# Experts of 98 tiles spread otherwise over three stages of a graph-network kernel: 43 pairs of tiles beside the gathers, 6 beside the softmax, none beside the combination

## The chip, the cores and the metric

The kernel runs on one core of one Trainium2 chip. The metric is the device time of one execution in microseconds (us); it is the median over several runs. Engines: PE (matrix multiplication), ACT (activation functions), DVE (elementwise vector work and scans), POOL (here mostly the issue of indirect gathers), SP (issue of transfers). Each runs its own instruction stream in order, and streams wait for each other on semaphores.

## The reference

12500 nodes with 256 features. A first layer sums weighted messages over 200000 edges and multiplies by a matrix; then comes a mixture of experts whose gates are made by graph attention over 131072 edges. Cut to what matters here:

```python
h = (x @ W_gat).reshape(M, HEADS, NUM_EXPERTS)          # 4 heads, 4 experts
e = leaky_relu(a_src[src] + a_dst[dst])                  # one per edge and head
ee = exp(e - segment_max(e, dst)[dst])
alpha = ee / segment_sum(ee, dst)[dst]
scores = layernorm(segment_sum(h[src] * alpha, dst) + b_gat).mean(heads)
w = softmax(top_k(scores, 2))
for ei in range(4):
    hh = gelu(x @ W1[ei] + b1[ei])                       # 256 -> 512
    out += g[ei] * (hh @ W2[ei] + b2[ei])                # 512 -> 256
```

All four experts are computed for all nodes, and the gates weigh them at the end. So the experts don't depend on the attention: they may run at any time between the first layer and the final combination.

## The kernel before, in words

The nodes lie in 98 tiles of 128 rows, which are worked in 49 pairs. `build` runs stages one after the other, each its own block with a barrier at its end: layer norm and planning; the first layer's weighted sums with the sort of the attention's edges; `attention_terms`; then the three that the change touches.

**The gather stage**, `gather_and_experts` (L1057 to L1381). POOL issues 1024 gathers of the attention's rows (L1144, 16 to a batch) and then 98 scatters (L1165). Beside it PE, ACT and DVE compute the experts of the first `EARLY_PAIRS` = 39 pairs: per pair and expert a first layer (L1236), Gelu on ACT (L1190), a second layer (L1247), the bias added by DVE (L1321), and a store of 256 KB to `y_dram` from ACT's queue (L1196).

**The softmax stage**, `segment_softmax` (L1384 to L1544). DVE works over the edges in their order by scans: maxima (L1492, L1501), differences, then it asks ACT for two exponentials (the semaphore `s_go`; ACT at L1437 and L1438) and goes on with the weighted sums (L1520, L1526, L1541). Twice DVE needs a carry across the 128 partitions, for which it asks PE to turn a small tile (`turn`, L1450 and L1453): once with 4 rows, `turn(0, HEADS)`, once with 20, `turn(1, ROWF)`. Beside it runs a second form of the experts, a lane made by `late_experts` (L879), for the next `SCAN_PAIRS` = 4 pairs. In this lane ACT does what DVE does in the gather stage (the normalisation at L917, the copies out of PSUM at L927 and L944), and the bias is multiplied in by PE (L1001, before the matmuls of L1003; the first layer is L991, its Gelu L936). The places at which ACT and PE serve DVE are fixed in their programs: ACT does pair 0 of the lane, then waits for DVE's request and does the exponentials, then pairs 1 to 3. PE does pair 0 with the first turn in it, pair 1, pair 2 with the second turn in it, pair 3. Within a pair the turn stands behind the first layer of expert 2 and ahead of the second layer of expert 1 (`between` in `tensor_pair`). The lane works ahead on PE: the first layers of the next pair's experts 0 and 1 are computed while ACT ends the pair before.

**The combination**, `combine` (L1547 to L1787). POOL gathers the sums of each node from `state_dram` (L1648, 98 gathers in three parts of 20, 20 and 58 tiles). For each part DVE makes the gates (L1707 to L1760), with three requests to ACT in it: an exponential (L1658), a square root (L1664), an exponential (L1669). Then it combines: for each pair 8 steps on DVE (L1769) over the four experts' results `ys` and the nodes' values `xs`, which SP loads ahead into 10 slots (L1599, L1600) and stores from (L1608). Ten pairs follow the first part, ten the second, 29 the third. Beside it a third lane, `last`, does the experts of the last 6 pairs, with ACT's requests put by hand between its steps (`places`). SP loads nothing before the lane's first two inputs have come (`wait_begun`), and it loads a late pair only when the lane has stored it (`wait_stored`).

On ACT each change between Gelu, exponential and square root shows in the trace as an ACT_TABLE_LOAD.

Of the kernel before, what the change touches and what calls it, by code (L numbers as in the profile page):

```python
# [45 lines left out]
FB = HID // P  # L46
PAIRS = TILES // 2
N2 = 2 * P
EARLY_PAIRS = 39
SCAN_PAIRS = 4  # L50
ROWF = HE + HEADS
STATE = HE + 2 * HEADS
BIG = 1.5e38
# [1003 lines left out]
def gather_and_experts(nc, sem, edge_index, m):  # L1057


    with ExitStack() as ctx:  # L1060
# [117 lines left out]
        def _(act):  # L1178
# [15 lines left out]
            def store(n, e, i):  # L1194
                act.wait_ge(s_yo, n + 1)
                act.dma_start(m.y_dram.rearrange("(t p) e f -> p t e f", p=P)[:, ds(i * 2, 2), e, :], yo[:, e, :, :]  # L1196
                              ).then_inc(s_st[e], 16)

            def pair(i, k, first=False, last=False):
                for e in range(EXPERTS):  # L1200
                    hidden(i * EXPERTS + e, e, first=first and e < 2)
                    if e == 0 and not last:
                        load(i + 2, k)
                    if e >= 1:
                        store(i * EXPERTS + (e - 1), e - 1, i)
                    elif not first:
                        store(i * EXPERTS - 1, EXPERTS - 1, i - 1)
# [3 lines left out]
            pair(0, 0, first=True)  # L1211
            with act.Fori(0, EARLY_PAIRS // 2 - 1) as u:
                for k in range(2):
                    pair(u * 2 + (k + 1), (k + 1) % 2)
            pair(EARLY_PAIRS - 2, 1, last=True)
            pair(EARLY_PAIRS - 1, 0, last=True)
            store(EARLY_PAIRS * EXPERTS - 1, EXPERTS - 1, EARLY_PAIRS - 1)
            for e in range(EXPERTS):
                act.wait_ge(s_st[e], 16 * EARLY_PAIRS)

# [3 lines left out]
        def _(pe):  # L1224
# [26 lines left out]
            def turn(i):  # L1251
                pe.wait_ge(s_yn, i + 1)
                if not isinstance(i, int) or i >= 1:
                    pe.wait_ge(s_yt, i)
                for t in range(2):
                    for h in range(HALVES):
                        q = pe.transpose(psY[:, h, t * P:(t + 1) * P], yn[:, t, h * P:(h + 1) * P], m.ident[:])
                q.then_inc(s_ty, 1)

            def pair(i, k, first=False):  # L1260
                for e in range(EXPERTS):
                    if e == 2 and not (isinstance(i, int) and i == EARLY_PAIRS - 1):
                        turn(i + 1)
# [120 lines left out]
def segment_softmax(nc, sem, m):  # L1384
# [3 lines left out]
    with ExitStack() as ctx:  # L1388
# [17 lines left out]
        psT, psB = psE[:, 0:2 * P], psE[:, 2 * P:3 * P]  # L1406
        lane = late_experts(nc, sem, ctx, m, "scan", EARLY_PAIRS, SCAN_PAIRS)

# [8 lines left out]
        block = ctx.enter_context(nc.Block())  # L1417
# [14 lines left out]

        @block.scalar
        def _(act):
            lane.scalar(act, 0, 1)
            act.wait_ge(s_go, 1)
            act.activation(decay[:], decay[:], ACT.Exp).then_inc(s_a, 1)  # L1437
            act.activation(by_head(states[:, :, HE:ROWF]), e[:], ACT.Exp).then_inc(s_a, 1)  # L1438
            act.wait_ge(s_go, 2)
            act.activation(tail[:, 1, 0:HEADS], tail[:, 1, 0:HEADS], ACT.Exp).then_inc(s_a, 1)  # L1440
            lane.scalar(act, 1, SCAN_PAIRS)
            lane.wait_stored(act, SCAN_PAIRS)

        @block.tensor
        def _(pe):
            def turn(n, w):

                pe.wait_ge(s_ask, 2 * n + 1)
                for k in range(2):
                    t = pe.transpose(psT[0:w, k * P:(k + 1) * P], tail[:, k, 0:w], m.ident[:])  # L1450
                t.then_inc(s_t, 1)
                pe.wait_ge(s_ask, 2 * n + 2)
                pe.transpose(psB[:, 0:w], carried[0:w, 0:P], m.ident[0:w, 0:w]).then_inc(s_t, 1)  # L1453

            lane.tensor_pair(pe, None, True)
            lane.tensor_pair(pe, 0, True, lambda: turn(0, HEADS))
            lane.tensor_pair(pe, 1, True)
            lane.tensor_pair(pe, 2, True, lambda: turn(1, ROWF))
            lane.tensor(pe, 3, SCAN_PAIRS)

        @block.vector
        def _(v):
# [84 lines left out]
def combine(nc, sem, b_gat, gamma, beta, out, m):  # L1547


    with ExitStack() as ctx:  # L1550
# [4 lines left out]
        SLOTS = 10  # L1555
        ROUNDS = PAIRS // SLOTS
        REST = PAIRS - ROUNDS * SLOTS
# [16 lines left out]
        ge = sb("f_ge", [P, T, EXPERTS])  # L1574
        ys = sb("ys", [P, SLOTS, 2, EXPERTS, FEAT])
        xs = sb("xs", [P, SLOTS, 2, FEAT])
        LATE = EARLY_PAIRS + SCAN_PAIRS
        lane = late_experts(nc, sem, ctx, m, "last", LATE, PAIRS - LATE)
        assert LATE >= PAIRS - REST

        s_c, s_clear = sem("f_const"), sem("f_states_cleared")
        s_got = [sem(f"f_gathered{n}") for n in range(PARTS)]
# [8 lines left out]
        block = ctx.enter_context(nc.Block())  # L1591

        @block.sync
        def _(sp):
            for n, a in enumerate((b_gat, gamma, beta)):
                sp.dma_start(vec[:, n, :], a.rearrange("(o c) -> o c", o=1).to_broadcast([P, HE])).then_inc(s_c, 16)

            def load(i, k):
                sp.dma_start(ys[:, k, :, :, :], y_t[:, ds(i * (2 * SLOTS) + 2 * k, 2), :, :]).then_inc(s_in[k], 16)  # L1599
                sp.dma_start(xs[:, k, :, :], x1_t[:, ds(i * (2 * SLOTS) + 2 * k, 2), :]).then_inc(s_in[k], 16)  # L1600

            def store(i, k):
                sp.wait_ge(s_done, i * SLOTS + (k + 1))
                if isinstance(i, int) and i * SLOTS + k == PAIRS - 1:
                    sp.dma_start(out_t[:, T - 2, :], xs[:, k, 0, :]).then_inc(s_out[k], 16)
                    sp.dma_start(out[FULL_TILES * P:NODES, :], xs[0:LAST_ROWS, k, 1, :]).then_inc(s_out[k], 16)
                else:
                    sp.dma_start(out_t[:, ds(i * (2 * SLOTS) + 2 * k, 2), :], xs[:, k, :, :]).then_inc(s_out[k], 16)  # L1608

            def refill(i, k):  # L1610
                sp.wait_ge(s_out[k], i * 16)
                if isinstance(i, int) and i * SLOTS + k >= LATE:
                    lane.wait_stored(sp, i * SLOTS + k - LATE + 1)
                load(i, k)

            def round_(i):

                fixed = isinstance(i, int)
                for k in range(SLOTS):
                    if fixed and i * SLOTS + k >= PAIRS:  # L1620
                        return
                    store(i, k)
                    if k >= 2 and not (fixed and (i + 1) * SLOTS + k - 2 >= PAIRS):
                        refill(i + 1, k - 2)
                    if k < 2 and not (fixed and (i == 0 or (i + 1) * SLOTS + k - 2 >= PAIRS)):
                        refill(i, SLOTS + k - 2)

            lane.wait_begun(sp)
            for k in range(SLOTS):
                if k == SLOTS // 2:  # L1630
                    sp.wait_ge(s_got[0], 16 * PART[1])
                load(0, k)
            round_(0)
            with sp.Fori(1, ROUNDS - 1) as i:
                round_(i)
            round_(ROUNDS - 1)
            round_(ROUNDS)
            for k in range(SLOTS):
                sp.wait_ge(s_out[k], 16 * (ROUNDS + (k < REST) + (k == REST - 1)))
# [12 lines left out]
        @block.scalar  # L1652
        def _(act):
            def weights(n):

                a, b = PART[n], PART[n + 1]
                act.wait_ge(s_go, 3 * n + 1)
                act.activation(w1[:, a:b, :], w1[:, a:b, :], ACT.Exp).then_inc(s_a, 1)  # L1658
                act.activation(w0[:, a:b, :], w0[:, a:b, :], ACT.Exp).then_inc(s_a, 1)

            def deviation(n):
                a, b = PART[n], PART[n + 1]
                act.wait_ge(s_go, 3 * n + 2)
                act.activation(one[:, 1, a:b], one[:, 1, a:b], ACT.Sqrt, bias=m.eps[:, 0:1]).then_inc(s_a, 1)  # L1664

            def gate(n):
                a, b = PART[n], PART[n + 1]
                act.wait_ge(s_go, 3 * n + 3)
                act.activation(ge[:, a:b, :], ge[:, a:b, :], ACT.Exp).then_inc(s_a, 1)  # L1669


            places = [[(0, 1), (0, 2), (0, 3)], [(1, 3), (2, 0), (2, 1)], [(3, 1), (3, 2), (3, 3)]]
            pairs = PAIRS - LATE
            between = [{} for _ in range(pairs)]
            for n in range(PARTS):
                for f, (u, place) in zip((weights, deviation, gate), places[n]):
                    between[u][place] = lambda f=f, n=n: f(n)
            lane.scalar_pair(act, None, True)
            for u in range(pairs):
                lane.scalar_pair(act, u, u < pairs - 1, between[u])  # L1680
            lane.wait_stored(act, pairs)

        @block.tensor
        def _(pe):
            lane.tensor(pe, 0, PAIRS - LATE)

        @block.vector
        def _(v):
# [122 lines left out]
```

## Time and profile before

| what | us |
|---|---|
| median of 3 runs (4309.44 to 4312.2) | 4310.04 |
| profiled execution, its own time | 4316.67 |
| its span, first to last instruction | 4315.1 |
| PE busy in the span | 3097.8 (72%) |
| POOL busy | 2801.6 (65%) |
| DVE busy | 1853.2 (43%) |
| ACT busy | 711.1 (16%) |

All times in rows are microseconds from the start of the span of one profiled execution, unless marked ns. In a line of the timeline stand: start, duration, engine, line of the kernel, operation, what it writes and reads, the number of instructions merged into it, and in brackets how long the engine had been idle and what ended that. In the view of stretches each engine has its busy time and, in brackets, its instructions, in the order PE, PE's weight loads, DVE, ACT, POOL; then come the granted clock of PE as a share of full speed, the share of DMA and its GB/s. Durations of matmuls overlap where several are merged. A row with DMA_INDIRECT on POOL is the issue of a gather, not its transfer.

### The profile page before, as it was taken

To read this page: it belongs to the slowest core of one execution; us is meant where nothing else is said; L and a number is where in the kernel's file an instruction comes from. 1 tells how busy PE (TensorE), PEld (TensorE's weight loads), DVE (VectorE), ACT (ScalarE), POOL (GpSimd) and SP (SyncE) were. 2 spreads that over 40 slices of the span, in tenths; PEclk is the share of its full clock that TensorE was granted. 3 is DMA by queue.
4 is the path that set the end of the run, shared out by engine and by line. 5 is a ranking of instruction groups with operands and counts; after the bars stand their busy time and mean duration, and the time that the engine had idled before them with its cause. 6 is when DMAs were issued, how large, how long until landed. Compare 5 with 4: busy or idle time off the path is not lost. (4 is left out here: it accounts for less than half of the span.)

```text
span 4315.1 us, 59490 instructions
## 1 busy us (share of the span) xinstructions
PE 3097.8 (72%) x13541; PEld 2436.0 (56%) x13542; DVE 1853.2 (43%) x4572; ACT 711.1 (16%) x1985; POOL 2801.6 (65%) x2958
## 2 busy tenths in 40 slices
PE   1356666677787887889979999999999400166846
PEld 0234444455555665666658888888888300144634
DVE  5233344534545456433333444444431000188648
ACT  4000000000111111122222222222222000031412
POOL 0677777777777777777747777777777777500860
PEclk6677778877878888998979999999999755588978
DMA  7533333333333433444422222222222110003749
GB/s 245 160 101 101 104 104 107 109 109 111 111 112 114 117 116 115 120 120 124 125 89 61 60 61 63 61 61 63 58 63 61 37 17 10 28 22 137 284 164 348
DMA packets 298222, 449.93 MB, mean 104 GB/s; under 512 B 61256, under 2 KB 232339, under 8 KB 297491
## 3 DMA queue, kind: packets, MB, share of 16 engines
q0 software_dynamic: 114144, 216.61, 19.2%
q1 hardware_dynamic: 83238, 137.78, 8.8%
q10 hardware_dynamic: 100749, 94.40, 6.7%
q8 instruction: 48, 0.79, 0.1%
q14 instruction: 43, 0.35, 0.0%
HBM read 330.48 MB, written 105.96 MB: 101 GB/s over the span
## 5 line engine op out<-in xcount | busy, mean ns | idle before, releaser
L519 POOL DMA_INDIRECT rows<-feats,idx x1564 | 1506.7, 963 | 546.6 <-issue 508.5
L665 PE MATMUL node_sums<-rows,hot 128*128 x3904 | 1122.3, 446 | 480.0 <-SPq L502 458.3
L665 PEld LDWEIGHTS node_sums<-rows,hot 128*128 128x128 f32 x3904 | 832.6, 221 | 728.5 <-issue 592.2
L1144 POOL DMA_INDIRECT got<-row_dram,d_idx x1024 | 994.4, 971 | 356.7 <-issue 306.1
L709 DVE TENSOR_SCALAR hot<-iota,rel,ew_t 128x128 f32<-128x128 f32 x1952 | 556.0, 362 | 64.7 <-DVE rel L705 1.9
L705 DVE TENSOR_SCALAR rel<-dst_t,step_base 128x4 f32 x488 | 123.6, 253 | 1061.3 <-PE node_sums L665 1005.9
L1236 PE MATMUL d_hidden<-d_yt,w 128*128 128x256 f32 x2496 | 569.0, 381 | 0.8 <-DVE d_yt L1336 0.8
L1247 PE MATMUL d_expert<-w,hid 128*128 128x256 f32 x2496 | 564.0, 379 | 0.0
L1247 PEld LDWEIGHTS d_expert<-w,hid 128*128 128x128 f32 x2496 | 474.2, 190 | 64.5
L1236 PEld LDWEIGHTS d_hidden<-d_yt,w 128*128 128x128 f32 x2496 | 470.5, 191 | 62.7 <-DVE d_yt L1336 1.2
L1321 DVE TENSOR_TENSOR yo<-d_expert,b2r 128x512 f32<-128x512 f32 x156 | 107.9, 692 | 708.5 <-PE d_expert L1247 708.5
L1190 ACT ACTIVATE hid<-d_hidden,b1c 128x256 f32<-128x256 f32 x624 | 261.9, 470 | 886.4 <-PE d_hidden L1236 882.0
L573 ACT COPY sums<-node_sums 128x256 f32<-128x256 f32 x98 | 36.5, 373 | 1770.6 <-PE sums_turned L657 1770.6
L980 PE MATMUL scan_ps_y_turned<-ident,scan_y 128*128 128x128 f32 x16 | 2.9, 313 | 371.4 <-ACT scan_y L917 371.4
L980 PEld LDWEIGHTS scan_ps_y_turned<-ident,scan_y 128*128 128x128 f32 x16 | 2.2, 160 | 372.1 <-ACT scan_y L917 371.8
L1648 POOL DMA_INDIRECT ns<-state_dram,last_pos x98 | 156.2, 1593 | 30.4 <-issue 29.6
L1311 DVE TENSOR_TENSOR hot_lo<-iota_b,lo 128x512 bf16<-128x512 bf16 x256 | 159.4, 693 | 0.0
L1769 DVE SCALAR_TENSOR_TENSOR xs<-ys,sc,xs 128x256 f32<-128x256 f32 x392 | 156.2, 480 | 5.6 <-DMA xs<-x_dram 5.0
L1481 DVE COPY decay<-adfirst 128x4 f32<-128x4 f32 x1 | 0.2, 166 | 369.0 <-DMA adfirst<-adst_dram,dst_first 369.0
L1644 POOL MEMSET ns<- 128x2352 f32 x1 | 2.1, 2057 | 237.0 <-POOLq L1388 237.0
L1311 DVE TENSOR_TENSOR hot_hi<-iota_b,hi 128x392 bf16<-128x392 bf16 x256 | 124.9, 562 | 0.0
L653 PE MATMUL x_product<-w_t,sums_t 128*128 128x256 f32 x400 | 124.8, 443 | 0.0
(295 smaller groups left out, 2861.4 us busy)
## 6 DMA issues: line engine op xcount, KB each, us to landing
ys<-y_dram SPq DMA_DIRECT2D x49, 1024.0 KB, 9.8
y_dram<-yo ACTq DMA_DIRECT2D x156, 256.0 KB, 2.2
rows<-feats,idx POOLq DMA_INDIRECT x1564
got<-row_dram,d_idx POOLq DMA_INDIRECT x1024
feats<-xout SPq DMA_DIRECT2D x14, 896.0 KB, 4.9
x_dram<-x ACTq DMA_DIRECT2D x98, 128.0 KB
xs<-x_dram SPq DMA_DIRECT2D x49, 256.0 KB, 10.6
x_ring<-in_x ACTq DMA_DIRECT2D x97, 128.0 KB
```

The lines of the kernel that those rows point to most:

```text
L519: pool.indirect_dma_start(rows[:, k, j, :], None, feats, bass.IndirectOffsetOnAxis(ap=idx[:, half, k, j:j + 1], axis=0)).then_inc(s_got[k] ...
L653: t = pe.matmul(psX[:, 0:FEAT], sums_t[:, k * P:(k + 1) * P], w_t[:, k, :], start=False, stop=(k == HALVES - 1))
L665: t = pe.matmul(psA[:, ds(((code >> 1) & 1) * 512, FEAT)], hot[:, r, j, :], rows[:, ds((code >> 2) & (RING - 1), 1), j, :], start=False, s ...
L705: v.tensor_scalar(rel[:, r, :], m.dst_t[:, ds(g * GT, GT)], m.step_base[:, ds(s, 1)], None, ALU.subtract).then_inc(s_rel, 1)
L709: t = v.tensor_scalar(hot[:, r, j, :], m.iota[:], rel[:, r, j:j + 1], m.ew_t[:, ds(g * GT + j, 1)], ALU.is_equal, ALU.mult)
L1144: pool.indirect_dma_start(got[:, k, j, 0:ROWF], None, m.row_dram, bass.IndirectOffsetOnAxis(ap=idx[:, k, j:j + 1], axis=0)).then_inc(s_got ...
L1190: t = act.activation(hid[:, e % 2, 2 * q + f, :], psL[(e % 2) * 2 + q][:, f, :], ACT.Gelu, bias=b1c[:, e, 2 * q + f:2 * q + f + 1])
L1236: t = pe.matmul(psL[(e % 2) * 2 + q][:, f, :], w1[:, h, e, (2 * q + f) * P:(2 * q + f + 1) * P], yt[:, k, h, :], start=(h == 0), stop=(h = ...
L1247: q = pe.matmul(psO[e % 2][:, t, :], hid[:, e % 2, f, t * P:(t + 1) * P], w2[:, f, e, :], start=(f == 0), stop=(f == FB - 1))
L1311: o = v.tensor_tensor(t[:, a:a + STRIP, :], iota_b[:, None, 0:wide].to_broadcast([P, STRIP, wide]), part[:, ds(q * HCOLS + a, STRIP)][:, : ...
L1648: pool.indirect_dma_start(ns[:, t, :], None, m.state_dram, bass.IndirectOffsetOnAxis(ap=m.last_pos[:, t:t + 1], axis=0), bounds_check=GEDG ...
L1769: q = v.scalar_tensor_tensor(xs[:, k, t, :], ys[:, k, t, e, :], sc[:, ds(i * (2 * SLOTS) + (2 * k + t), 1), e], xs[:, k, t, :], ALU.mult, ...
```

## The change

`EARLY_PAIRS` goes from 39 to 43 and `SCAN_PAIRS` to the rest, 6. The lane of the combination is taken out, with SP's two kinds of waits for it, and ACT serves the gates of each part directly. In the softmax stage ACT now does two pairs ahead of the exponentials (`lane.scalar(act, 0, 2)`) and four behind them; PE does pair 0 with the first turn, pairs 1 to 3, pair 4 with the second turn, and pair 5.

```diff
-EARLY_PAIRS = 39
-SCAN_PAIRS = 4
+EARLY_PAIRS = 43
+SCAN_PAIRS = PAIRS - EARLY_PAIRS
...
         @block.scalar
         def _(act):
-            lane.scalar(act, 0, 1)
+            lane.scalar(act, 0, 2)
             act.wait_ge(s_go, 1)
             act.activation(decay[:], decay[:], ACT.Exp).then_inc(s_a, 1)
             act.activation(by_head(states[:, :, HE:ROWF]), e[:], ACT.Exp).then_inc(s_a, 1)
             act.wait_ge(s_go, 2)
             act.activation(tail[:, 1, 0:HEADS], tail[:, 1, 0:HEADS], ACT.Exp).then_inc(s_a, 1)
-            lane.scalar(act, 1, SCAN_PAIRS)
+            lane.scalar(act, 2, SCAN_PAIRS)
             lane.wait_stored(act, SCAN_PAIRS)
...
             lane.tensor_pair(pe, None, True)
             lane.tensor_pair(pe, 0, True, lambda: turn(0, HEADS))
-            lane.tensor_pair(pe, 1, True)
-            lane.tensor_pair(pe, 2, True, lambda: turn(1, ROWF))
-            lane.tensor(pe, 3, SCAN_PAIRS)
+            lane.tensor(pe, 1, 4)
+            lane.tensor_pair(pe, 4, True, lambda: turn(1, ROWF))
+            lane.tensor(pe, 5, SCAN_PAIRS)
...
-        LATE = EARLY_PAIRS + SCAN_PAIRS
-        lane = late_experts(nc, sem, ctx, m, "last", LATE, PAIRS - LATE)
-        assert LATE >= PAIRS - REST
...
                 sp.wait_ge(s_out[k], i * 16)
-                if isinstance(i, int) and i * SLOTS + k >= LATE:
-                    lane.wait_stored(sp, i * SLOTS + k - LATE + 1)
                 load(i, k)
...
-            lane.wait_begun(sp)
             for k in range(SLOTS):
...
-            places = [[(0, 1), (0, 2), (0, 3)], [(1, 3), (2, 0), (2, 1)], [(3, 1), (3, 2), (3, 3)]]
-            pairs = PAIRS - LATE
-            between = [{} for _ in range(pairs)]
             for n in range(PARTS):
-                for f, (u, place) in zip((weights, deviation, gate), places[n]):
-                    between[u][place] = lambda f=f, n=n: f(n)
-            lane.scalar_pair(act, None, True)
-            for u in range(pairs):
-                lane.scalar_pair(act, u, u < pairs - 1, between[u])
-            lane.wait_stored(act, pairs)
-
-        @block.tensor
-        def _(pe):
-            lane.tensor(pe, 0, PAIRS - LATE)
+                weights(n)
+                deviation(n)
+                gate(n)
```

## Rows read from the trace of the kernel before

**Rows 1.** Busy time by stage: stage, its us, busy per engine, granted clock, DMA share.

```profile
2240.00:3389.00 1149.00, 1147.05 (x6177) 1011.46 (x6175) 438.58 (x793) 261.92 (x624) 850.53 (x911) 1.00 0.24 61
3389.00:3741.00 352.00, 0.00 (x0) 0.00 (x0) 0.53 (x1) 0.00 (x0) 257.16 (x299) 0.51 0.08 12
...
3751.00:3989.00 238.00, 149.60 (x598) 111.56 (x598) 208.49 (x146) 58.80 (x97) 1.00 (x1) 0.80 0.21 84
3989.00:4315.00 326.00, 220.50 (x888) 165.50 (x888) 216.12 (x545) 88.85 (x168) 158.21 (x99) 0.83 0.72 263
```

**Rows 2.** The same view: two equal stretches of the gather stage.

```profile
3200.00:3380.00 180.00, 179.03 (x844) 157.42 (x843) 27.49 (x52) 41.98 (x100) 131.53 (x147) 1.00 0.24 60
3400.00:3580.00 180.00, 0.00 (x0) 0.00 (x0) 0.00 (x0) 0.00 (x0) 131.81 (x146) 0.50 0.10 17
```

**Rows 3.** Timeline around the first request to ACT: start, us, engine, line, [idle<-releaser].

```profile
3816.65 0.59 ACT L944 COPY scan_expert_out<-scan_ps_expert 128x512 f32<-128x512 f32 x1 [4.51 <-PE scan_ps_expert L1003]
...
3817.81 1.28 ACT L1437 ACT_TABLE_LOAD   x1 [0.57 <-ACT scan_expert_out L944]
...
3829.94 3.62 ACT L1437 ACTIVATE decay<-decay 128x4096 f32<-128x4096 f32 x1 [10.85 <-DVEq L1512]
...
3843.92 17.22 DVE L1520 TENSOR_TENSOR states<-states 128x16384 f32<-128x16384 f32 x1 [5.91 <-ACT tail L1440]
3843.93 1.28 ACT L936 ACT_TABLE_LOAD   x1
3845.22 3.03 ACT L936 ACTIVATE scan_hidden<-scan_ps_hidden,b1c 128x256 f32<-128x256 f32 x8
...
3847.99 3.57 PE L1003 MATMUL scan_ps_expert<-w,scan_hidden 128*128 128x256 f32 x8
...
3852.11 1.99 PE L1003 MATMUL scan_ps_expert<-w,scan_hidden 128*128 128x256 f32 x8
```

**Rows 4.** Timeline of the rest of the softmax stage.

```profile
3876.78 0.59 ACT L944 COPY scan_expert_out<-scan_ps_expert 128x512 f32<-128x512 f32 x1 [4.51 <-PE scan_ps_expert L1003]
...
3889.02 3.62 PE L991 MATMUL scan_ps_hidden<-scan_y_turned,w 128*128 128x256 f32 x16
...
3915.97 0.60 PE L1450 MATMUL e_turn<-ident,tail 128*20 128x128 f32 x2 [23.33 <-DVEq L1467]
...
3933.69 46.57 DVE L1541 TENSOR_TENSOR_SCAN states<-decay,states 128x256 f32<-128x256 f32 x60
...
3973.20 0.59 ACT L944 COPY scan_expert_out<-scan_ps_expert 128x512 f32<-128x512 f32 x1 [4.51 <-PE scan_ps_expert L1003]
...
3989.43 2.06 POOL L1644 MEMSET ns<- 128x2352 f32 x1 [237.02 <-POOLq L1388]
```

**Rows 5.** Timeline of ACT in the combination: one copy in successive pairs, undisturbed.

```profile
4221.38 0.59 ACT L944 COPY last_expert_out<-last_ps_expert 128x512 f32<-128x512 f32 x1 [3.28 <-PE last_ps_expert L1003]
...
4256.02 0.59 ACT L944 COPY last_expert_out<-last_ps_expert 128x512 f32<-128x512 f32 x1 [4.26 <-PE last_ps_expert L1003]
```

**Rows 6.** Timeline of the combination: the first burst on DVE and the gathers.

```profile
4041.03 31.75 DVE L1769 SCALAR_TENSOR_TENSOR xs<-ys,sc,xs 128x256 f32<-128x256 f32 x80
...
4044.27 29.39 POOL L1648 DMA_INDIRECT ns<-state_dram,last_pos  x1 [0.30 <-issue]
```

**Rows 7.** Timeline of DVE in the combination: gates of the second and third part.

```profile
4077.86 0.27 DVE L1707 TENSOR_TENSOR seg_keep<-ns,has_edges 128x80 f32<-128x80 f32 x1 [5.08 <-DMA ns<-state_dram,last_pos]
...
4179.16 0.40 DVE L1707 TENSOR_TENSOR seg_keep<-ns,has_edges 128x232 f32<-128x232 f32 x1 [51.44 <-DMA ns<-state_dram,last_pos]
...
4211.72 0.40 DVE L1757 TENSOR_TENSOR f_ge<-f_ge,src_sorted 128x232 f32<-128x232 f32 x1 [3.73 <-ACT f_ge L1669]
```

**Rows 8.** DMA of the last 103 us: GB/s in 40 slices; queue, packets, MB.

```profile
GB/s 0 0 288 362 381 339 424 399 401 414 403 400 408 397 411 389 410 414 390 420 401 403 408 403 411 402 402 410 398 415 408 395 417 404 395 417 377 383 158 6
...
q10 hardware_dynamic: 2176, 2.10, 5.8%
```

**Rows 9.** Waits of the same stretch: us in total, times, longest.

```profile
DVE xs L1769 <- DMA xs<-x_dram: 5.0, 7, 1.2
```

## The prediction

> **What bounds the kernel now.** I read the stages first: busy time per engine in the stretches between the barriers [rows 1]. From the gather stage on there are three, and each has its own limit. In the gather stage PE does the experts of 39 pairs in 1149 us (29.5 us a pair) and then does nothing for 352 us, while POOL issues gathers to the end: POOL sets its length. In the softmax stage (238 us) DVE is busy 208 us and everything else much less, so DVE's chain of scans sets it, with whatever DVE has to wait for. In the combination (326 us) no engine is full; there one must look at what DVE waits for, which is the timeline's to tell [rows 6, 7].
>
> The question for each moved pair is therefore not how much work it is, since that is the same everywhere, but which queue it stands in and what waits behind it.
>
> **Gather stage: four more pairs, cost 0.** Four pairs at 29.5 us are 118 us on PE, which is idle for the last 352 us of the stage [rows 1]; ACT and DVE are idle there too. Could they slow POOL? Two stretches of 180 us show 147 POOL instructions with 131.53 us busy beside the experts and 146 with 131.81 us alone [rows 2]. That is no difference, so I take 0 and keep 2 us as the upper end (one instruction in 146, over 118 us, would be under 1 us; I double it for the stores). Below zero nothing is possible: POOL gains nothing from it. The stage would still have over 230 us of idle PE as cover.
>
> **Softmax stage, first part: one pair now stands ahead of the exponentials.** Before, ACT does one pair, then waits for DVE's request. Its last copy of that pair starts at 3816.65, the table load for the exponential at 3817.81, and the exponential itself only at 3829.94, after 10.85 us of waiting for DVE [rows 3]. So ACT was early by 10.85 us. The change puts a second whole pair in between. How long is a pair of this lane? Not 29.5 us, since it also multiplies the bias in on PE; the same copy of two successive pairs, with no request between them, lies 4256.02 - 4221.38 = 34.64 us apart [rows 5]. The copy that ends the second pair thus starts at 3816.65 + 34.64 = 3851.29. From the copy's start to the table load's end are 3817.81 + 1.28 - 3816.65 = 2.44 us [rows 3], so the exponential starts at 3853.7 in place of 3829.94: **23.8 us later**. DVE has nothing to do meanwhile: already before it waited 5.91 us for ACT there [rows 3], and all its later steps of this stage follow from the exponentials. In short: a pair's 34.64 minus ACT's slack of 10.85. The lower bound is 20.7 us, from the nearest shorter row, 31.6 us from the first hidden block to the last copy in the pair after the exponentials (3876.78 - 3845.22, with two blocks already done ahead); the upper is 26, if PE starts the pair slowly (eight matmuls in 3.57 us in place of 1.99 [rows 3], some more of them).
>
> The Trainium skill (page "ScalarE: Activation LUTs", section "What ACT_TABLE_LOAD costs") states about 2.66 us for a switch of table, 1.38 us of it a drain; the rows show 1.28 us and an ACTIVATE 0.01 us behind the load [rows 3], with no drain. By the page the delay would be 25.2 us, by the rows 23.8; the measurement decides.
>
> **Softmax stage, second part: DVE's question to PE comes while PE is busy.** PE turns DVE's tails for it at a fixed place in its program: after the third layer-1 block of a pair. Before, that was the second pair after the exponentials. PE was ready at 3889.02 + 3.62 = 3892.64 and DVE asked at 3915.97, so PE waited 23.33 us for DVE [rows 4]. Now the turn stands in pair 4, the third pair after the exponentials. The pair after the exponentials (pair 2 now) ends with its copy at 3876.78 + 23.8 = 3900.6; pair 3 takes 34.64 more, to 3935.2; from the copy to the end of the third block are 3892.64 - 3876.78 = 15.86 us, so PE reaches the turn at 3951.1. DVE asks at 3915.97 + 23.8 = 3939.8. So DVE now waits **11.3 us** more: PE's 23.3 us of slack minus one pair of 34.64. Together the softmax stage grows by 35.1 us.
>
> Is DVE's chain still what ends the stage? Its last scan ended at 3933.69 + 46.57 = 3980.26, ACT's last copy started at 3973.20 [rows 4]. Behind the turn both programs are as before (the rest of one pair, then the last pair), so both move by 35.1 and keep their distance of 7 us. The combination's first instruction goes from 3989.43 [rows 4] to about 4024.5.
>
> **Combination: six pairs leave, gain 8 us.** This stage looks like the place to win, since 6 pairs of PE work and their transfers go. But its path runs through POOL. DVE's first part of gates waits for 20 gathers; a burst of 80 combining steps follows, 31.75 us; during it one gather on POOL takes 29.39 us, and it ends 0.9 us behind the burst [rows 6]. The second round shows the same pattern, so there are two such stalls. DVE waited 5.08 us for gathers before the second gates, and 51.44 us before the third [rows 7]. A burst that starts earlier stops POOL earlier for as long, so the third gates still start when 98 gathers and two stalls are over: same distance from the stage's start. What the experts delayed in the first two parts is swallowed by these two waits: gain 0.
>
> Two things remain. In the third gates DVE waited 3.73 us for an exponential that stood behind an expert's copy on ACT [rows 7]; about 0.5 us must stay (the 0.40 us exponential and its semaphore), so 3.2 us are won. Then 29 pairs are combined to the end with DMA at some 405 GB/s [rows 8] and DVE waiting 5.0 us for loads, 7 times [rows 9]. The experts' stores there are 2.10 MB [rows 8], 2.10 / 0.405 = 5.2 us of transfer, and no more than DVE's 5.0 us of waits can be won. Sum 3.2 + 5.0 = 8.2; I take 8, with 3 as the lower end (nothing of the waits) and 12 as the upper (the start of the stage gets its loads earlier and something of it lasts).
>
> **The sum.** Gather 0, softmax +23.8 + 11.3, combination -8: **+27.1 us**. The profiled execution took 4316.67 us (span 4315.1, the rest lies around it), so it would be 4343.8; the median of the runs is 6.6 us lower at 4310.04, which makes 4337. A measurement of this kernel can tell about 0.2% (8.6 us) from no change. The ends: softmax 32 to 38 (twice a pair of 33 to 36 us, less the two slacks of 10.85 and 23.33), gather 0 to 2, combination -12 to -3, so 4330 to 4347; the corners will hardly meet, so 4331 to 4344 is the forecast's own range.
>
> **Rivals.**
> (a) *Only the first delay counts.* If PE gets to the turn no later than DVE asks, the 11.3 us go and 23.8 - 8 = 15.8 remain: 4326. For it: this step is a difference of two estimated times. Against: it needs a pair in PE's 23.33 us of slack [rows 4] in place of 34.64.
> (b) *Faster: the stalls of POOL were made by the transfers.* Place: the two gathers of 29 us [rows 6]. If they come from full DMA queues, and lifting the experts' traffic frees them, the third gates start as soon as the second burst is over, 51.44 us earlier [rows 7]: 35.1 - 8 - 51.4 = -24.3, so 4286. It decides from 36 of the 51 us on. Against: the stall ends with the burst, within 1 us, and the loads of the experts' results, which are most of the traffic, stay.
> (c) *No change: DVE's chain has cover in the softmax.* If the requests to ACT and PE were off the path that ends the stage, only -8 would be left: 4302, within 0.2%. Against: before the first exponential ACT waited for DVE, and behind the last one DVE for ACT [rows 3], so the chain passes through both. That the change doesn't do what it says gives the same time: that would be the pair ahead of the exponentials overlapping with DVE's work after all.
> (d) *PE at its lower clock.* After a pause the eight matmuls of L1003 took 3.57 us, later 1.99 [rows 3]. The granted clock over the softmax stage is 0.80 [rows 1], between the levels 1.2 and 2.4 GHz. If pair 1 and pair 3 run half at the lower level, each gains 34.64 x 0.8 / 2 = 14 us; both are on the path: 4365. Against: PE idles less than before, not more.
>
> **How the numbers follow.** Forecast 0.75; (a) 0.12, (b) 0.04, (c) 0.04, (d) 0.05. The range takes in the forecast's and (a)'s times, 4325 to 4345, and leaves out (b), (c), (d) and the forecast's far corners. Slower: forecast, (a), (d) = 0.92; same: (c) 0.04; faster: (b) 0.04.
>
> **What would show it.** In the profile of the changed kernel: the exponential of the softmax stage with no wait of ACT for DVE before it, 24 us later relative to the stage's start; DVE waiting some 11 us for PE at the second turn, where PE waited before; some 273 us for the stage in place of 238; in the combination two stalls of about 29 us on POOL as before and the third gates 190 us from its first instruction; no wait for loads in the last pairs. POOL's rate beside the experts unchanged, and PE busy until about 3507 us. The prediction is wrong if the stalls shrink, if the turn finds PE waiting, or if the gathers' stage grows.

## The result and the profile after

The changed kernel took 4342.05 us (median of 4, 4339.08 to 4344.24) against 4311.02 us (4309.44 to 4312.2; four runs, one more than the prediction had): a ratio of 1.0072, 95% interval 1.0054 to 1.0089. So it is slower by 31 us, with 23 to 38 us inside the interval. The forecast was 4337, range 4325 to 4345. The profiled execution took 4339.08 us.

First the stages. Stretches between the barriers of the changed kernel, with the columns of [rows 1]:

```profile
2240.00:3389.00 1149.00, 1148.03 (x6191) 1013.12 (x6190) 438.06 (x792) 263.06 (x628) 850.61 (x911) 1.00 0.27 61
3389.00:3500.00 111.00, 108.53 (x509) 95.22 (x507) 15.49 (x26) 25.14 (x60) 80.99 (x92) 1.00 0.27 61
3500.00:3741.00 241.00, 0.00 (x0) 0.00 (x0) 0.00 (x0) 0.00 (x0) 173.45 (x206) 0.51 0.07 8
3748.00:4020.00 272.00, 215.68 (x894) 162.79 (x894) 208.50 (x146) 80.73 (x144) 0.99 (x1) 0.89 0.22 83
4020.00:4337.00 317.00, 0.00 (x0) 0.00 (x0) 215.48 (x545) 12.42 (x19) 157.21 (x99) 0.50 0.67 246
```

PE now works on in the gather stage to about 3500 us and is idle for the last 241 us; before, it was idle for 352 [rows 1]. POOL's busy time in that stage is within 3 us of what it was (1105 us, before 1108). The softmax stage got longer, the combination shorter, and PE is not used in it at all.

The lengths of the stages come from the first instruction of each: POOL's L1126 at 2228.69 us (before 2232.25), the gather L1430 at 3748.00 (before 3751.41), and POOL's clearing of `ns` (L1638 now) at 4020.68.

| stage | before | after | forecast of the difference | measured |
|---|---|---|---|---|
| ahead of the gather stage | 2232.3 | 2228.7 | 0 | -3.6 |
| gather | 1519.2 | 1519.3 | 0 | +0.1 |
| softmax | 238.0 | 272.7 | +35.1 | +34.7 |
| combination, to the span's end | 325.7 | 316.4 | -8 | -9.3 |

The timeline of the softmax stage, the places that answer to [rows 3]:

```profile
3847.82 0.58 ACT L944 COPY scan_expert_out<-scan_ps_expert 128x512 f32<-128x512 f32 x1 [4.44 <-PE scan_ps_expert L1003]
...
3849.10 1.28 ACT L1437 ACT_TABLE_LOAD   x1 [0.70 <-ACT scan_expert_out L944]
3850.40 3.62 ACT L1437 ACTIVATE decay<-decay 128x4096 f32<-128x4096 f32 x1
...
3854.05 4.42 DVE L1515 TENSOR_TENSOR decay<-decay,seg_keep 128x4096 f32<-128x4096 f32 x1 [27.54 <-ACT decay L1437]
```

The exponential (L1437) follows its table load at once: no wait for DVE, where ACT had waited 10.85 us. DVE waits for it, 27.54 us before L1515 (before, 3.74). Measured from the stage's start the exponential comes at 3850.40 - 3748.00 = 102.4 us, before at 3829.94 - 3751.41 = 78.5: 23.9 us later (forecast 23.8).

And the second turn, on DVE, beside [rows 4]:

```profile
3935.80 0.23 DVE L1532 TENSOR_SCALAR cin<-tail,whole 128x4 f32<-128x4 f32 x1
...
3947.91 0.41 DVE L1469 COPY tail_t<-e_turn 20x256 f32<-20x256 f32 x1 [11.60 <-PE e_turn L1450]
...
3964.94 46.57 DVE L1541 TENSOR_TENSOR_SCAN states<-decay,states 128x256 f32<-128x256 f32 x60
```

DVE waits 11.60 us for PE's turned tile; the first turn of the same kernel, for which nobody is late, costs DVE 0.74. So 10.9 us are new (forecast 11.3).

The combination, beside [rows 7]:

```profile
4108.56 0.24 DVE L1691 TENSOR_TENSOR seg_keep<-ns,has_edges 128x80 f32<-128x80 f32 x1 [7.97 <-DMA ns<-state_dram,last_pos]
...
4209.42 0.40 DVE L1691 TENSOR_TENSOR seg_keep<-ns,has_edges 128x232 f32<-128x232 f32 x1 [51.46 <-DMA ns<-state_dram,last_pos]
...
4238.77 0.40 DVE L1741 TENSOR_TENSOR f_ge<-f_ge,src_sorted 128x232 f32<-128x232 f32 x1 [0.52 <-ACT f_ge L1663]
```

From the stage's start the third gates begin at 4209.42 - 4020.68 = 188.7 us (before 189.7), and DVE's wait ahead of them is 51.46 us as before. The wait for the last exponential (L1741) is down from 3.73 to 0.52 us. POOL is still stopped twice:

```profile
4072.47 28.98 POOL L1642 DMA_INDIRECT ns<-state_dram,last_pos  x1 [0.30 <-issue]
...
4129.84 28.99 POOL L1642 DMA_INDIRECT ns<-state_dram,last_pos  x1 [0.30 <-issue]
```

### The profile page after: what moved, and what is told of

Same layout as the page of the kernel before. It is cut to its first block and busy times, and to the rows that moved or that the text cites. A ratio compares the mean times of both kernels' runs of the same rounds, so it can differ in the third digit from the quotient of the medians.

```text
span 4337.1 us, 59587 instructions
## 1 busy us (share of the span) xinstructions
PE 3038.5 (70%) x13477; PEld 2407.6 (56%) x13478; DVE 1868.4 (43%) x4600; ACT 682.3 (16%) x1947; POOL 2798.8 (65%) x2958
## 5 line engine op out<-in xcount | busy, mean ns | idle before, releaser
L1236 PE MATMUL d_hidden<-d_yt,w 128*128 128x256 f32 x2752 | 626.8, 381 | 0.8 <-DVE d_yt L1336 0.8
L1247 PE MATMUL d_expert<-w,hid 128*128 128x256 f32 x2752 | 621.9, 379 | 0.0
L1247 PEld LDWEIGHTS d_expert<-w,hid 128*128 128x128 f32 x2752 | 522.9, 190 | 71.1
L1236 PEld LDWEIGHTS d_hidden<-d_yt,w 128*128 128x128 f32 x2752 | 518.8, 191 | 69.1 <-DVE d_yt L1336 1.2
L1321 DVE TENSOR_TENSOR yo<-d_expert,b2r 128x512 f32<-128x512 f32 x172 | 119.0, 692 | 804.9 <-PE d_expert L1247 804.9
L1190 ACT ACTIVATE hid<-d_hidden,b1c 128x256 f32<-128x256 f32 x688 | 288.2, 470 | 972.4 <-PE d_hidden L1236 972.4
L1638 POOL MEMSET ns<- 128x2352 f32 x1 | 2.1, 2058 | 271.7 <-POOLq L1388 271.7
L1165 POOL DMA_INDIRECT adst_first<-sdat,sidx x98 | 96.3, 982 | 38.2 <-issue 26.9
```

Source lines behind the costliest of these rows:

```text
L1190: t = act.activation(hid[:, e % 2, 2 * q + f, :], psL[(e % 2) * 2 + q][:, f, :], ACT.Gelu, bias=b1c[:, e, 2 * q + f:2 * q + f + 1])
L1236: t = pe.matmul(psL[(e % 2) * 2 + q][:, f, :], w1[:, h, e, (2 * q + f) * P:(2 * q + f + 1) * P], yt[:, k, h, :], start=(h == 0), stop=(h = ...
L1247: q = pe.matmul(psO[e % 2][:, t, :], hid[:, e % 2, f, t * P:(t + 1) * P], w2[:, f, e, :], start=(f == 0), stop=(f == FB - 1))
```

## The experiments

Twelve runs, each beside the kernel before on the same chip. They fell on four chips, and on two of these the kernel before takes about 5800 us and not 4310, with the same program. Ratios of runs on different kinds of chip must not be mixed; so each experiment names the time of the kernel before. Where a delay of some 10 or 20 us is asked for, the ratio alone says little, since its interval on the slower chips is some 17 to 22 us wide; the length of the stage in the trace carries the reading.

**One delay at a time.** The first run takes from the change only ACT's second pair ahead of the exponentials, with 39, 4 and 6 pairs as before:

```diff
-            lane.scalar(act, 0, 1)
+            lane.scalar(act, 0, 2)
...
-            lane.scalar(act, 1, SCAN_PAIRS)
+            lane.scalar(act, 2, SCAN_PAIRS)
```

> The kernel before, with one thing of the change alone: ACT does two pairs of the softmax lane ahead of the exponentials, two behind them. Theory (a pair's 34.6 us less ACT's slack of 10.9, and PE's turn still waits for DVE): +23.8 us, so a ratio of 1.0055, the combination unchanged. Rival (the exponentials are covered by other work of DVE): no difference, 1.000.

Measured: ratio 1.0052 (1.0034 to 1.0071), before 5810 us; by the medians 27.7 us. POOL's wait through the softmax stage in the trace of this run, and ACT's rows in it:

```profile
L1644 POOL MEMSET ns<- 128x2352 f32 x1 | 2.1, 2059 | 263.4 <-POOLq L1388 263.4
```

```profile
5311.58 1.28 ACT L1437 ACT_TABLE_LOAD   x1 [0.70 <-ACT scan_expert_out L944]
5312.87 3.62 ACT L1437 ACTIVATE decay<-decay 128x4096 f32<-128x4096 f32 x1
```

POOL has nothing to do between its first instruction of the softmax stage and the combination, so its idle time, 263.4 us, is the stage's length. In the order of before it is 237.2 us on this chip (the trace of 45/4/0 below) and 237.02 in [rows 4]: +26.2 us. The rival (exponentials covered) is out.

The second run moves only PE's second turn by one pair:

```diff
-            lane.tensor_pair(pe, 1, True)
-            lane.tensor_pair(pe, 2, True, lambda: turn(1, ROWF))
-            lane.tensor(pe, 3, SCAN_PAIRS)
+            lane.tensor(pe, 1, 3)
+            lane.tensor_pair(pe, 3, False, lambda: turn(1, ROWF))
```

> The kernel before, with the other thing alone: PE's second turn stands in the last of the four pairs, one pair later. Theory (34.6 us of a pair less PE's slack of 23.3): DVE waits 11.3 us for the turn, +11.3 us, ratio 1.0026. Rival (only the first delay counts): 1.000. Second rival (two delays overlap in the changed kernel and each alone is larger): over +15.

Measured: ratio 1.0026 (1.0011 to 1.0041), before 5810 us; by the medians 11.1 us. POOL's wait through the stage, and ACT's exponential:

```profile
L1643 POOL MEMSET ns<- 128x2352 f32 x1 | 2.1, 2057 | 250.0 <-POOLq L1388 250.0
```

```profile
5254.52 3.62 ACT L1437 ACTIVATE decay<-decay 128x4096 f32<-128x4096 f32 x1 [8.47 <-DVEq L1511]
```

+12.8 us, with the exponentials where they were (78.6 us from the stage's start, before 78.5). Rival (a), that only the first delay counts, is out.

Why 26.2 and not 23.8 in the first run? ACT's slack is not a constant of the kernel. With the lane's order of before it was 10.85 us in [rows 3], 8.47 here, and 8.20, 10.92 and 7.87 in the three traces of 45/4/0 below (here the last two of them):

```profile
5445.45 3.62 ACT L1437 ACTIVATE decay<-decay 128x4096 f32<-128x4096 f32 x1 [10.92 <-DVEq L1512]
...
3831.53 3.62 ACT L1437 ACTIVATE decay<-decay 128x4096 f32<-128x4096 f32 x1 [7.87 <-DVEq L1512]
```

The second pair keeps its length (5310.30 - 5275.66 = 34.64 in the first run), but the last copy of the lane's first pair comes 65.2 to 69.0 us after the stage's start: 65.2 in [rows 3] and in the changed kernel, 67.8 in the first run. These 2.5 us more are what the first run lost beyond the forecast. It doesn't go with the kind of chip: the slack of 7.87 was seen where the kernel before takes 4316 us, that of 10.92 where it takes 5802. Why the first pair ends earlier or later was not tried. The changed kernel and its variants with the same softmax stage show both delays together: in six traces the exponentials come 23.9 to 27.7 us later, and DVE waits 10.8 to 11.1 us more at the second turn. On this chip the changed kernel lost 272.6 - 237.2 = 35.4 us (trace below), less than 26.2 + 12.8, with a first pair that ended after 65.8 us; both delays are on the path.

**The combination's part alone.** 45 pairs beside the gathers, the softmax stage as before with 4, none beside the combination:

```diff
-EARLY_PAIRS = 43
+EARLY_PAIRS = 45
...
-            lane.scalar(act, 0, 2)
+            lane.scalar(act, 0, 1)
...
-            lane.tensor(pe, 1, 4)
-            lane.tensor_pair(pe, 4, True, lambda: turn(1, ROWF))
-            lane.tensor(pe, 5, SCAN_PAIRS)
+            lane.tensor_pair(pe, 1, True)
+            lane.tensor_pair(pe, 2, True, lambda: turn(1, ROWF))
+            lane.tensor(pe, 3, SCAN_PAIRS)
```

(against the changed kernel). It ran three times, and the changed kernel twice more. First, on the chip of the two runs above:

> The combination's part of the change alone: 45 pairs beside the gathers, the softmax stage word for word as before with 4 pairs, none beside the combination. Theory (softmax cost is all of the loss, combination gains 8 to 9, two more pairs beside the gathers cost nothing): -9 us, ratio 0.998. Rival (stores and loads of 45 pairs slow the gathers): 0 or slower, with a longer gather stage.

> The changed kernel unaltered, beside the three others. The three changed stages of the two traces differ by 25.4 us in sum, the medians by 31. Theory (chance between executions, outside these stages): ratio 1.006 to 1.007, that is +25 to +29. Rival (a cost outside the changed stages): 1.0072 again, and the sum of x1, x2 and x3 (+26) falls short of it by 5 us.

Measured, before 5810 us: 45/4/0 at 1.0218 (1.0197 to 1.024), the changed kernel at 1.0177 (1.0158 to 1.0196). Both expectations missed by far: by the medians 45/4/0 is 118 us slower where 9 us faster was expected, and nothing in the trace of before let one expect it. What the changed kernel's run was to tell, whether a cost lies outside the changed stages, it could not tell here. The trace of the changed kernel on this chip, stretches of its gather stage (from 2655 to 5307 us):

```profile
3000.00:3500.00 500.00, 99.45 (x191) 48.61 (x191) 12.77 (x23) 8.38 (x20) 343.45 (x380) 0.50 0.12 19
3500.00:4000.00 500.00, 97.81 (x188) 47.24 (x188) 14.08 (x26) 8.38 (x20) 340.68 (x378) 0.50 0.12 19
...
4300.00:4700.00 400.00, 400.00 (x2231) 353.40 (x2230) 170.59 (x311) 90.47 (x216) 0.00 (x0) 1.00 0.13 44
```

For 500 us at a time PE executes some 190 matmuls, then, without any change in its program, 2231 in 400 us. The timeline where the one turns into the other:

```profile
4086.57 0.94 POOL L1144 DMA_INDIRECT got<-row_dram,d_idx  x1 [0.30 <-issue]
4087.20 0.59 PE L1247 MATMUL d_expert<-w,hid 128*128 128x256 f32 x1 [2.21 <-issue]
4087.81 0.95 POOL L1144 DMA_INDIRECT got<-row_dram,d_idx  x1 [0.30 <-issue]
...
4090.00 0.59 PE L1247 MATMUL d_expert<-w,hid 128*128 128x256 f32 x1 [2.21 <-issue]
...
4092.80 0.59 PE L1247 MATMUL d_expert<-w,hid 128*128 128x256 f32 x1 [2.21 <-issue]
...
4094.91 4.42 PE L1247 MATMUL d_expert<-w,hid 128*128 128x256 f32 x10 [1.52 <-issue]
```

Each single matmul of 0.6 us stands behind 2.2 us of idle time that nothing in the profile explains ("issue"), until some 7 us after POOL has begun the last of its 1024 gathers (4087.81); from 4094.91 on there are ten in 4.4 us. The granted clock, 0.50 in the slow stretch, doesn't make the gaps: the matmul itself takes only 0.6 us of each 2.8. POOL's own gathers still follow one another every 1.25 us. The same holds for the combination, where the lane stood beside gathers: from L1644 (5472.4 us) to the span's end (5845.1) the first run, with the lane, takes 372.7 us, 45/4/0 without it 5925.9 - 5597.8 = 328.1. So on this chip the engines beside POOL hardly advance while it issues gathers, the 43 pairs are done mostly behind the gathers, and PE ends the stage at 5307 us, with POOL idle before it (875 us ahead of its scatters, which need DVE's plan, and 213.8 ahead of L1430). There every pair moved into this stage costs its full time. The stages of the traces: gather 2546.1 us with 39 pairs (first run), 2662.6 with 43, 2707.8 with 45. That is 29 us a pair for the first four and 27 for all six; the second run, with the same 39 pairs as the first, shows 2535.5, so such a figure is good to 2 or 3 us. For 45/4/0 the stages add up: 162 us more in the gather stage and 45 less in the combination than the first run, 117 against the 118 of the medians over before.

Then both again on another chip, and all 49 pairs beside the gathers:

> 45 pairs beside the gathers, 4 beside the softmax in the order of before, none beside the combination, once more: on the chip of the first four runs the kernel before itself took 5810 us, and PE came to the end of the gather stage long after POOL. Theory: where POOL sets the gather stage (the kernel before near 4310 us), the gather stage keeps its 1519 us, the softmax stage its 238, the combination loses 9: -9 us, ratio 0.998. Where PE sets it (before near 5810), two pairs more than in the changed kernel cost 59 us more: ratio 1.02 as in the first call. Rival (more pairs beside the gathers cost time on any chip): slower than before in both.

> The changed kernel again. Theory: near 4310 us of before, ratio 1.006 to 1.0072, the three stages +0, +35, -9. Where before takes 5810: 1.0177 again.

> All 49 pairs beside the gathers, no experts later. Theory where POOL sets the gather stage: 49 pairs of 29.5 us are 1446 us, 73 us less than the stage, so it still costs nothing; softmax stage 238 less nothing (no wait of DVE for the lane was there before), combination -9: ratio 0.998, the same as y1. Rival (PE idle through the softmax runs DVE's turns at a low clock): a few tenths of a us more in the softmax stage. Rival (PE ends after POOL): slower by the excess.

Measured, before 5802 us, a second chip of this kind: 1.0206 (1.0175 to 1.0236), 1.018 (1.0151 to 1.0209), and 1.0404 (1.0373 to 1.0435) for 49/0/0. For the first two that is what was expected where PE sets the stage; for 49/0/0 it is the rival in which PE ends after POOL. In the trace of 49/0/0 POOL waits for the end of that stage and then through the softmax stage:

```profile
L1429 POOL DMA_INDIRECT adfirst<-adst_dram,dst_first x1 | 1.0, 1000 | 381.3 <-POOLq L1060 381.3
...
L1631 POOL MEMSET ns<- 128x2352 f32 x1 | 2.1, 2057 | 236.9 <-POOLq L1388 236.9
```

381.3 us idle ahead of L1429, with every one of the 49 pairs in the stage; but 236.9 us of softmax stage, the length of before, with no experts in it. The gather stage on this chip takes 2647.9 us with 43 pairs, 2719.1 with 45 and 2818.7 with 49: 28.5 us a pair over the six.

The third run of 45/4/0 fell on a chip where the kernel before takes 4316 us:

> 45 pairs beside the gathers, the softmax stage as before with 4, none beside the combination: on a third chip. If the kernel before takes about 4310 us here, PE is idle at the end of the gather stage, and theory says -9 us, ratio 0.998, third gates 189 us from the combination's start with two stalls of 29 us. If it takes about 5800 as on the two chips of the earlier runs, PE is starved beside the gathers and each of the six extra pairs adds its 27 to 29 us: ratio 1.021.

Measured: 4310.03 against 4315.81, ratio 0.9988 (0.9978 to 0.9998). Here the expectation holds in the trace, and more pairs beside the gathers don't cost time on every chip: gather stage 3752.8 - 2233.5 = 1519.3 us with 45 pairs, softmax 3991.0 - 3752.8 = 238.2, combination 4306.9 - 3991.0 = 315.9. DVE ahead of the second and third gates:

```profile
4078.94 0.24 DVE L1691 TENSOR_TENSOR seg_keep<-ns,has_edges 128x80 f32<-128x80 f32 x1 [7.97 <-DMA ns<-state_dram,last_pos]
...
4179.75 0.40 DVE L1691 TENSOR_TENSOR seg_keep<-ns,has_edges 128x232 f32<-128x232 f32 x1 [51.45 <-DMA ns<-state_dram,last_pos]
```

The third gates stand 188.7 us from the stage's start, as in the changed kernel. So the combination's gain (-9.8) and the softmax stage's loss (+35) are separate, and the first can be had without the second. Last, on a chip with before at 4310:

> All 49 pairs beside the gathers, no experts later. If the kernel before takes about 4310 us here: 49 pairs of 29.5 us are 1446 us, the gather stage stays at 1519; softmax 238 (the lane never held DVE up there); combination 316: -9 us as with 45 pairs, ratio 0.998. Rival (the pairs beside the last gathers or the scatters lengthen the stage): over 1519 us, no gain. If the kernel before takes about 5800: 1.040 again.

```diff
-EARLY_PAIRS = 43
+EARLY_PAIRS = 49
...
-            lane.scalar(act, 0, 2)
...
-            lane.scalar(act, 2, SCAN_PAIRS)
-            lane.wait_stored(act, SCAN_PAIRS)
...
+            turn(0, HEADS)
+            turn(1, ROWF)
```

(the softmax lane goes entirely). Measured: 4303.8 against 4310.18, ratio 0.9984 (0.9975 to 0.9993). Two stretches of its gather stage, as in [rows 1]:

```profile
2240.00:3389.00 1149.00, 1148.04 (x6193) 1013.16 (x6193) 439.73 (x795) 263.60 (x628) 849.76 (x913) 1.00 0.26 61
3389.00:3741.00 352.00, 275.37 (x1294) 242.12 (x1292) 38.25 (x65) 65.48 (x156) 253.00 (x294) 0.90 0.20 47
```

PE is busy 275 of the last 352 us and still done before POOL; the stage takes 1518.7 us. The low clock of an idle PE (0.50 granted there) costs nothing in the softmax stage: it takes 238.0 us, and the turns' matmuls 0.59 and 0.60 us as before. This version beats both kernels on such chips, by a little (6.4 us against before), and is the worst of all on the other kind.

**Who sets the gather stage.** One run with every second gather left out, and half of the attention's rows with them; the experts are all there:

```diff
-                sp.wait_ge(s_got[k], i * (16 * GB) + 16 * GB)
+                sp.wait_ge(s_got[k], i * (8 * GB) + 8 * GB)
...
-                for j in range(GB):
+                for j in range(0, GB, 2):
```

> The changed kernel with every second of the 1024 gathers of the attention left out (so its result is not the reference's); all experts stay. It asks what makes PE slow beside the gathers where the kernel takes 5800 us. Theory (as long as POOL issues gathers the other engines get an instruction through only every 0.7 to 2.8 us): the slow stretch is halved from 1430 to about 720 us, in the rest PE runs at 29.5 us a pair, and the gather stage shrinks from 2662 to about 2000 us. Rival (PE slow by itself for some other cause in this stage, such as its clock): the stage keeps its 2662. Where the kernel before takes 4310: POOL no longer sets the stage, PE does, with 43 x 29.5 = 1269 us in place of 1519.

Measured: 4095.53 us, before 4316. The gather stage takes 3503.5 - 2230.0 = 1273.5 us; worked out were 1269. This is the floor that PE sets with 43 pairs, 246 us under POOL's. This is one run. It fell on a chip where PE isn't starved, so it says nothing on what starves PE on the others; that stays open.

**What stops POOL in the combination.** The changed kernel with each combining step cut to 16 of 256 columns, so the rest of the combination is left out; transfers and waits are all kept:

```diff
-                    q = v.scalar_tensor_tensor(xs[:, k, t, :], ys[:, k, t, e, :],
+                    q = v.scalar_tensor_tensor(xs[:, k, t, 0:16], ys[:, k, t, e, 0:16],
                                                sc[:, ds(i * (2 * SLOTS) + (2 * k + t), 1), e],
-                                               xs[:, k, t, :], ALU.mult, ALU.add)
+                                               xs[:, k, t, 0:16], ALU.mult, ALU.add)
```

> The changed kernel, each combining step of DVE cut to 16 of its 256 columns, so the combination of the other columns is left out; all loads, stores and waits stay. It asks what stops POOL's gathers for 29 us. Theory (DVE's long bursts of these steps): no gather over 5 us, DVE's wait ahead of the third gates shrinks, third gates some 130 us from the stage's start in place of 189. Rival (the DMA traffic of the loads and stores): both stalls of about 29 us stay.

Measured: 5871.44 us, before 5802. On this chip the full kernel shows no stopped gather either (the longest of its 98 takes 1.25 us), so it told nothing. Once more, on another:

> The changed kernel, each combining step of DVE cut to 16 of its 256 columns, so the combination of the other columns is left out; all loads, stores and waits stay. It asks what stops two of POOL's gathers for 29 us, on a chip where they are stopped. Theory (DVE's long bursts): the stops shrink with the burst, to under 15 us each, and the third gates come under 165 us from the stage's start in place of 189. Rival (the DMA traffic of loads and stores): both stops of 29 us stay. Where the kernel before takes 5800 us no gather is stopped and the run tells nothing on this.

Measured: 4278.23 us, before 4310. All 98 gathers in one row (least, median, greatest ns), and DVE at the third gates:

```profile
L1642 POOL DMA_INDIRECT ns<-state_dram,last_pos x98: 992/997/1192, 4021.4 to 4148.4; - x98
```

```profile
4066.68 11.84 DVE L1753 SCALAR_TENSOR_TENSOR xs<-ys,sc,xs 128x16 f32<-128x16 f32 x80
...
4150.60 0.40 DVE L1691 TENSOR_TENSOR seg_keep<-ns,has_edges 128x232 f32<-128x232 f32 x1 [33.09 <-DMA ns<-state_dram,last_pos]
```

The longest gather takes 1.19 us beside a burst of 80 steps in 11.84 us; DVE's wait ahead of the third gates falls from 51.46 to 33.09, and they come 4150.60 - 4018.53 = 132.1 us from the stage's start in place of 188.7. The transfers were all there, only earlier: from 4067 to 4096 us DMA moved 342 GB/s beside gathers of 1.0 us each, more than the 304 GB/s beside the first stopped gather of the changed kernel (4072 to 4100). So it is DVE's steps that stop POOL, not the traffic: rival (b) is out. That the stops go entirely and don't just shrink is what the first of the two expectations had (no gather over 5 us, third gates at some 130 us); the second, with under 15 and under 165 us, asked for less. Whether it is the length of the single step or of the train that does it was not tried.

## Why the prediction was right, and where it was off

**Gather stage, 0.** Measured +0.1 us, and still 0 with 45 and 49 pairs, on the chips with before near 4310. It was right for the reason given: PE's floor is 1273.5 us with 43 pairs, POOL's 1519. It is right there alone, and that the result was taken on such a chip was luck: on two other chips the same change costs about 100 us. There PE sets the stage, and each pair moved into it costs 27 to 29 us. The range of 0 to 2 us rested on one trace of one chip, and its cover was not there on every chip.

**Exponentials one pair later, +23.8.** Measured 23.9. The term is the pair's 34.64 us less ACT's slack, and the mechanism holds: ACT goes straight from the second pair to the exponentials. That the size agrees to 0.1 us is partly luck. The first pair ended 65.2 us from the stage's start in both traces; in other traces it ended up to 3.8 us later, and the delay was up to 27.7 us, above the 26 that the prediction gave as this term's upper end.

**Second turn, +11.3.** Measured 10.9 in the changed kernel and 12.8 alone. The turn found PE busy where PE had waited 23.33 us, as worked out.

**Table load.** 3849.10 + 1.28 = 3850.38, and the exponential starts at 3850.40. The load was now on the path and cost 1.28 us, with no drain behind it. The larger figure of the Trainium skill (page "ScalarE: Activation LUTs", section "What ACT_TABLE_LOAD costs") would have put the delay at 25.2 us; the trace has 23.9. Since the delay varies between traces, the better sign is the gap behind the load, 0.02 us here and 0.01 in the first run (5311.58 + 1.28, exponential at 5312.87): the trace shows no drain.

**Combination, -8.** Measured -9.3. The part of it that was the point: the third gates keep their distance from the stage's start (188.7 us, before 189.7), since the gathers and DVE's two bursts set it and the experts hardly did. The 3.73 us wait shrank to 0.52 as expected, and DVE's waits for loads in the last stretch went from 5.0 us to 0.41 (8 steps at 4330.20). With the third gates 1.0 us earlier, for which the prediction had 0, that is 8.8 of the 9.3 us.

**The sum.** The three stages show +25.5 us, worked out were 27.1; the medians differ by 31. A gap of some 5 us is left. It is not clear of noise, since 25.5 lies within the interval of 23 to 38, and it is not settled. The one profiled execution of before was 5.7 us slower than its median, that of after 3 us faster. The part ahead of the gather stage, the same code in all, ended anywhere from 2226.7 to 2233.5 us in six traces near 4310. But the two better versions also gained less than their stages say (5.8 us for 9.4, 6.4 for 9.5), so a cost of 3 to 5 us that goes with taking the lane out of the combination is possible. Some 0.4 us of it can be seen: an execution takes 1.5 us more than its span with the lane and 1.7 to 2.1 without, mostly 1.9 or more. A second profile of the kernel before on such a chip would tell more; there is none.

The rivals: (a) fell to the second run, (b) to the changed kernel's own trace, in which both stops stay with the experts' traffic gone, and then to the short steps, (c) to both single delays, (d) to the trace, in which the pairs in question keep their 34.6 us (3847.82 - 3813.18 = 34.64 for the copy that ends a pair).

## What to carry to other kernels

Work that is off the critical path is not placed by how much of it fits beside a stage, but by what waits behind it in its engine's queue: 2 pairs more in the softmax stage cost 34.7 us although PE and ACT were idle for over a third of it, because each request of the bound engine found one more pair ahead of it. A slack is spent once: a pair of 34.6 us against slacks of 10.9 and 23.3 us gives the two delays directly, before anything is run. But a slack read from one execution is one sample: this one was 10.9 us in the trace that was read and 7.9 to 10.9 in others of the same order. And a cover measured on one chip should be tried on another before it is built on.

## What the runs showed that was not expected

On two of the four chips of the experiments the unaltered kernel took 5800 us in place of 4310. While POOL issued indirect gathers, PE got 188 to 199 matmuls through in 500 us on both, against 2231 in 400 us when POOL was quiet, and DVE's combining steps stood apart by about 1.4 us in place of 0.4 while gathers ran beside them. In return POOL was never stopped by DVE's bursts on those chips. On the others it was the other way round: PE ran at full rate beside the gathers, and each of DVE's first two bursts of 80 steps stopped one gather for 29 us. What makes the difference between the chips was not found.

There one gather waited through some 71 successive steps of DVE, 29 us, and went on 0.9 us after the last. The Trainium skill (page "SBUF — State Buffer", section "Who interferes with whom") says that a DVE instruction with two inputs in SBUF contends with a GpSimd instruction that reads SBUF, for one port pair that goes to whichever starts first, for the whole of one instruction. The combining steps have two inputs in SBUF; that the issue of a gather is such a read is not shown here. The trace agrees only in that the one waits for the other: beside the first eight steps of the burst two gathers got through, in 1.05 and 1.28 us, then the third was held for far longer than one step of 0.4 us, and 80 steps of 16 columns stopped nothing.
